# Causal row maxima as whole-array matmuls, one head at a time, beside scores in halves of the array

## What is computed

```python
x = x + layernorm(attention(layernorm(x)))
x = x + layernorm(moe(layernorm(x)))      # 8 experts, 2 per token

# attention, 16 heads of 16 channels, latent keys of 64
c_kv  = x @ W_dkv.T
q_lat = einsum('bhtd,hdl->bhtl', q, k_eff)
attn  = softmax(causal(q_lat @ c_kv.T / 4))
y     = (attn @ c_kv) @ v_eff
```

## Time and profile before

| | us |
|---|---|
| median of 3 runs (lowest, highest) | 1520.93 (1519.54, 1530.33) |
| profiled execution | 1524.09 |
| its span in the profile | 1522.4 |
| mean granted TensorE clock | 0.805 |

### The profile page before, as it was taken

The page is one execution under the profiler, slowest core; times in us unless marked ns, Lnnn a source line. Parts: engine busy times, 40 slices in busy tenths (PEclk is TensorE's granted clock), DMA queues, the critical chain, the costliest instruction groups (busy, mean ns, idle before and its releaser), DMA issues. The chain is left out here.

```text
span 1522.4 us, 26952 instructions
## 1 busy us (share of the span) xinstructions
PE 1097.4 (72%) x8321; PEld 771.1 (51%) x8322; DVE 812.4 (53%) x2076; ACT 644.2 (42%) x1112; POOL 526.3 (35%) x544
## 2 busy tenths in 40 slices
PE   6843678888888888889872350799999999998000
PEld 3421344344434434444322350799899899998000
DVE  4522656655665666555507851455455555555255
ACT  3430045554554555455562441344344444444322
POOL 3100045544554454444454776100000000000785
PEclk9985579988996898777895555899999999999555
DMA  4974225533553445443342124423441432411324
GB/s 154 282 199 144 93 71 183 178 133 126 184 187 106 153 148 178 149 151 109 130 174 113 55 73 148 157 64 137 153 156 48 153 118 81 155 41 48 94 85 152
DMA packets 109100, 200.27 MB, mean 132 GB/s; under 512 B 27396, under 2 KB 76948, under 8 KB 100756
## 3 DMA queue, kind: packets, MB, share of 16 engines
q1 hardware_dynamic: 96488, 143.74, 29.0%
q0 software_dynamic: 12544, 55.62, 10.2%
HBM read 109.38 MB, written 89.42 MB: 131 GB/s over the span
## 5 line engine op out<-in xcount | busy, mean ns | idle before, releaser
L782 ACT ACTIVATE att_pt<-att_ps_s 128x1024 f32<-128x1024 f32 (+3 forms) x384 | 293.9, 813 | 270.6 <-PE att_ps_s L700 269.3
L812 DVE TENSOR_REDUCE att_pm<-att_ps_m 128x1 f32<-128x512 f32 (+1 forms) x512 | 306.5, 650 | 183.6 <-PE att_ps_m L652 110.9
L1430 ACT ACTIVATE moe_hf<-moe_ps_h,moe_b 128x256 f32<-128x256 f32 x288 | 137.2, 476 | 237.3 <-PE moe_ps_h L1381 232.1
L596 POOL TENSOR_SCALAR_AFFINE_SELECT att_pt<-att_pt 128x512 f32<-128x512 f32 x128 | 80.9, 638 | 321.7 <-ACT att_pt L782 321.7
L652 PE MATMUL att_ps_m<-att_k,att_q 50*128 50x512 f32 (+3 forms) x576 | 174.2, 437 | 21.3 <-DVE att_pm L812 11.1
L700 PE MATMUL att_ps_s<-att_q,att_k 50*128 50x512 f32 (+3 forms) x576 | 137.5, 443 | 41.5 <-ACT att_pt L782 30.9
L717 PE MATMUL att_ps_o<-att_pt,att_v 128*17 128x512 f32 (+3 forms) x1152 | 142.3, 618 | 8.1 <-POOL att_pt L596 4.3
L1456 DVE TENSOR_TENSOR moe_hTl<-moe_hf,moe_hTh 128x256 fp32r<-128x256 f32 x288 | 122.6, 426 | 9.8
L700 PEld LDWEIGHTS att_ps_s<-att_q,att_k 50*128 50x128 f32 x576 | 62.7, 198 | 122.8 <-issue 63.8
L652 PEld LDWEIGHTS att_ps_m<-att_k,att_q 50*128 50x128 f32 x576 | 90.5, 212 | 67.0 <-DVE att_pm L812 50.9
L586 POOL TENSOR_TENSOR att_rec<-att_sums,att_minus 128x16 f32<-128x16 f32 x33 | 96.0, 2909 | 39.1 <-ACT att_sums L768 39.1
(11 more groups left out here) (195 smaller groups left out, 2483.9 us busy)
## 6 DMA issues: line engine op xcount, KB each, us to landing
att_raw<-in_w SPq DMA_DIRECT2D x16, 1024.0 KB, 6.0
ws<-att_raw_hi SPq DMA_DIRECT2D x16, 1024.0 KB, 4.2
ws<-att_raw SPq DMA_DIRECT2D x16, 1024.0 KB, 6.7
ys<-att_zeros SPq DMA_DIRECT2D x16, 640.0 KB, 7.3
moe_rows<-xs SPq DMA_DIRECT2D x38, 256.0 KB, 2.7
ys<-moe_o SPq DMA_DIRECT2D x36, 256.0 KB, 2.2
weights_w_0h<-ws POOLq DMA_DIRECT2D x8, 1024.0 KB, 7.6
weights_w_0l<-ws POOLq DMA_DIRECT2D x8, 1024.0 KB, 10.1
```

The costliest lines, as they stand in the source:

```text
L782: act.activation(pt[:, blk % NPT, 2 * p:2 * p + 2, off:CH], ps_s[k % 2][:, :, off:CH], ACT.Exp, scale=HS ** -0.5).then_inc(ex_done, 1)
L812: return dve.tensor_reduce(pm[:, g % 2, place, h:h + 1], src, AX.X, ALU.max)
L1430: act.activation(hf[:, f % NHB], ps_h[f % NHB][:], ACT.Relu, bias=b1[r][:, f:f + 1]).then_inc(hf_done, 1)
```

## The change

- k has one tile per head (`[P, GH, T]` instead of `[P, 2, T]`), with the other head's 64 rows and the unused rows zero. q stays two heads to a tile, so one matmul over all 128 rows gives one head's products. All q and k slots are zeroed once: slot 0 in `project` (GpSimd q, VectorE k), slots 1 to 3 by GpSimd at the start of `attend`. SP waits for `init` of a slot before it loads into it.
- A unit is one matmul per piece and head over 128 rows, and its mask one bf16 matmul, identity 128 x 128 by 128 columns.
- Units are dealt one by one, by a cost per step. The turn goes from step 17 to step 16.
- Scores keep their two halves, reading k at `2 * p + e`.
- `xf` is no longer held during attention; its four loads are issued by SP in `route`, one after the other, and `residual` waits for each.

The steps that have units, before (pairs) and after, counted through both planners: before, steps 0, 1, 2, 5, 7 to 11, 13 to 17, 19, 20 and 22, with ten units in steps 14 to 17; after, steps 0, 2, 3, 4, 6, 7, 8, 10, 11, 12, 14, 15, 16, 18, 19, 20, 22 and 23, with four units in steps 14 to 17 and nine in 22, 23 and 0.

```diff
@@ add_slot
-    slots["k"].append(s.sb(f"k{g}", [P, 2, T], F32R))
+    slots["k"].append(s.sb(f"k{g}", [P, GH, T], F32R))
@@ load_group
-                         (kg[r:r + 2 * HS, h // 2, :], ks[:, c]), (kg[r + 2 * HS:r + KR, h // 2, :], ks[0, c])):
+                         (kg[r:r + 2 * HS, h, :], ks[:, c]), (kg[r + 2 * HS:r + KR, h, :], ks[0, c])):
@@ project
+                                                  (slots["q"][0][:].bitcast(F32), 0.0))):
...
+                dve.memset(slots["k"][0][:].bitcast(F32), 0.0).then_inc(slots["init"][0], 1)
@@ bank_jobs
+MATMUL, VALUES, SWITCH, MASK = 0.235 / CH, 0.44 / CH, 0.2, 0.125
...
+    work = [("unit", 1, m) for m in range(HALF, NU)] + [("unit", 2, m) for m in range(HALF)]
+    cost = [unit_keys(m) * MATMUL + len(UNITS[m][0]) * MASK * any(k0 + keys == (i + 1) * P for i, k0, keys, _ in UNITS[m][1])
+            for _, _, m in work]
+    taken = [2 * (CH - past(k)) * MATMUL for k in range(NS)]
+    for k in range(1, NS, 4):
+        taken[k] += SWITCH + sum((CH - past(2 * (blk % NB))) * VALUES for blk in (k // 2 - 2, k // 2 - 1))
+    even = (sum(taken) + sum(cost)) / NS
+    room = [max(0, even - t) for t in taken]
...
-    out[17] += [("turn", 1, 0), ("turn", 1, 1)]
+    out[16] += [("turn", 1, 0), ("turn", 1, 1)]
@@ attend, sync
                 for g in range(1, NSL):
+                    sp.wait_ge(slots["init"][g], 2)
                     load_ones(sp, d, slots, g)
...
-                        if g == 1:
-                            sp.dma_start(keep["xf"][:, bass.ds(b * TB, TB)],
-                                         d["x"][bass.ds(b * T, T), :].rearrange("(k p) c -> p k c", p=P)
-                                         ).then_inc(xf_in, 16)
@@ attend, gpsimd
+                for g in range(1, NSL):
+                    pool.memset(qg[g][:].bitcast(F32), 0.0).then_inc(slots["init"][g], 1)
+                    pool.memset(kg[g][:].bitcast(F32), 0.0).then_inc(slots["init"][g], 1)
@@ attend, tensor: unit replaces units
+                        for h in heads:
                             diag = k0 + keys == (i + 1) * P
...
+                            ins = pe.matmul(out[:, end:end + keys], qg[slot][:, h // 2, i * P:(i + 1) * P],
+                                            kg[slot][:, h, k0:k0 + keys], start=True, stop=not diag)
+                            end += keys
                             if diag:
...
+                                ins = pe.matmul(out[:, end - P:end], identb[:], future[:], start=False, stop=True)
@@ scores
-                        ins = pe.matmul(out[:, e, off:CH], kg[slot][rows, p, j * P:(j + 1) * P],
+                        ins = pe.matmul(out[:, e, off:CH], kg[slot][rows, 2 * p + e, j * P:(j + 1) * P],
@@ route, sync and vector
+                for b in range(B):
+                    sp.dma_start(xf[:, b * TB:(b + 1) * TB], d["x"][b * T:(b + 1) * T, :].rearrange("(k p) c -> p k c", p=P)
+                                 ).then_inc(xf_in, 16)
+                    sp.wait_ge(xf_in, b * 16 + 16)
...
                 def residual(b):
+                    dve.wait_ge(xf_in, b * 16 + 16)
```

More of the change, by code:

```diff
@@ L412, in unit_keys, with past @@
     return len(heads) * sum(keys for _, _, keys, _ in pieces)
+MATMUL, VALUES, SWITCH, MASK = 0.235 / CH, 0.44 / CH, 0.2, 0.125
+def past(k):
+    c, j, _ = STEPS[k]
+    return max(0, (j - c * TC) * P)
 def bank_jobs():
-    work = [("unit", 1, m) for m in range(HALF, NU, 2)] + [("unit", 2, m) for m in range(0, HALF, 2)]
-    cost = [2 * unit_keys(m) + 128 for _, _, m in work]
-    width = [CH - max(0, (j - c * TC) * P) + 96 for c, j, _ in STEPS]
+    work = [("unit", 1, m) for m in range(HALF, NU)] + [("unit", 2, m) for m in range(HALF)]
[6 more added lines that the diff above has]
+    room = [max(0, even - t) for t in taken]
     out, step, done = [[] for _ in STEPS], 0, 0
-    for (kind, more, m), c in zip(work, cost):
-        while step < NS - 1 and (done + c / 2) / sum(cost) > sum(width[:step + 1]) / sum(width):
+    for job, c in zip(work, cost):
+        while step < NS - 1 and (done + c / 2) / sum(cost) > sum(room[:step + 1]) / sum(room):
             step += 1
-        out[step] += [(kind, more, m), (kind, more, m + 1)]
+        out[step].append(job)
         done += c
@@ L634, in free, with unit @@
                         pe.wait_ge(bank_read[n % NBK], turns(b, n))
-                def units(b, g, m, n):
-                    pieces = UNITS[m][1]
+                def unit(b, g, m, out):
+                    heads, pieces = UNITS[m]
                     slot = g % NSL
@@ L641, in units @@
                         pe.wait_ge(loaded[slot], at(b, g // NSL * NSL, LOADS, NSL * LOADS + ONES))
-                    at_col, last = 0, [None, None]
+                    end = 0
                     for i, k0, keys, _ in pieces:
-                        for pair in range(len(UNITS[m][0])):
+                        for h in heads:
                             diag = k0 + keys == (i + 1) * P
-                            end = at_col + keys
-                            for e in range(2):
-                                h = UNITS[m + e][0][pair]
-                                rows = slice(64 * e, 64 * e + KM)
-                                if at_col == 0:
-                                    free(b, n + e)
-                                last[e] = pe.matmul(ps_m[(n + e) % NBK][:, at_col:end], qg[slot][rows, h // 2, i * P:(i + 1) * P],
-                                                    kg[slot][rows, h // 2, k0:k0 + keys], start=True, stop=not diag)
-                            if diag:
-                                for z in range(2):
-                                    for e in range(2):
-                                        rows = slice(64 * e, 64 * e + 64)
-                                        col = end - P + z * (P // 2)
-                                        last[e] = pe.matmul(ps_m[(n + e) % NBK][:, col:col + P // 2], pick[rows, z], future[rows, z],
-                                                            start=False, stop=z == 1)
-                            at_col = end
-                    for e in range(2):
-                        last[e].then_inc(bank_made[(n + e) % NBK], 1)
+                            ins = pe.matmul(out[:, end:end + keys], qg[slot][:, h // 2, i * P:(i + 1) * P],
+                                            kg[slot][:, h, k0:k0 + keys], start=True, stop=not diag)
+                            end += keys
+                            if diag:
+                                ins = pe.matmul(out[:, end - P:end], identb[:], future[:], start=False, stop=True)
+                    return ins
                 def max_turn(b, g, half, out):
@@ L681, in jobs @@
                     for (kind, more, m), n in todo:
-                        if kind == "unit":
-                            if m % 2 == 0:
-                                units(b, g + more, m, n)
-                            continue
                         free(b, n)
-                        do = {"turn": max_turn, "out": turn_out}[kind]
+                        do = {"unit": unit, "turn": max_turn, "out": turn_out}[kind]
                         do(b, g + more, m, ps_m[n % NBK]).then_inc(bank_made[n % NBK], 1)
@@ L1585, in build @@
         keep = {"ident": s.sb("ident", [P, P]), "passed": s.sem("passed"),
-                "pick": s.sb("pick", [P, 2, P], BF16), "future": s.sb("future", [P, 2, P // 2], BF16)}
+                "identb": s.sb("identb", [P, P], BF16), "future": s.sb("future", [P, P], BF16)}
         keep["y"] = s.sb("y", [P, B * NG + 1, TB, GH * HS])
-        keep["xf"] = s.sb("xf", [P, TILES, C])
         with ExitStack() as inner:
-            slots = {part: [] for part in ("q", "k", "v", "loaded")}
+            slots = {part: [] for part in ("q", "k", "v", "loaded", "init")}
             add_slot(slots, Store(nc, inner, "slots"), 0)
@@ L1595, in build @@
             attend(nc, d, keep, slots)
+        keep["xf"] = s.sb("xf", [P, TILES, C])
         keep["wgt"] = s.sb("wgt", [P, 3, TILES])
@@ L1617 @@
     w = {k.replace("L0_attn_", "").replace("L0_ffn_", ""): np.asarray(a) for k, a in inputs.items()}
-    half = P // 2
-    pick = np.zeros((half, 2, P), np.float32)
-    future = np.zeros((half, 2, half), np.float32)
-    pick[:, 0, :half] = np.eye(half)
-    future[:, 0] = np.triu(np.full((half, half), -1e30), 1)
-    pick[:half - 1, 1, half:P - 1] = np.eye(half - 1)
-    pick[half - 1, 1, :half] = 1.0
-    future[:, 1] = future[:, 0]
-    future[half - 1, 1] = -1e30
+    future = np.triu(np.full((P, P), -1e30, np.float32), 1)
     arrays = {
```

23 lines of the change are left out of this document (12 added, 11 removed).

## The result

The changed kernel takes 1536.05 us (median of 15 runs, 1532.67 to 1545.41), the kernel before 1527.99 on the same chips (median of 15, 1519.54 to 1533.86). The ratio is 1.0064, 95% interval 1.0043 to 1.0084: slower by 0.4 to 0.8%, less than the 1% by which the prediction counts a change. The forecast was 1531.0 against 1520.9, +0.66%.

A forecast was written before the change was run, and what follows sets the result against it. No one engine is full: TensorE carries the chain, ScalarE and VectorE hold it up in turn. From 1524.1 us, loop 0, start +6.0, routing +4.5 give 1534.6; the median is 3.2 lower, 1531; range 1482 to 1573.

The forecast's parts named there:

- Change 1: Attention loop: whole-row units cost TensorE 8.5 us a group, 4.2 more than before, and masks 3.8, 1.2 more.
- whole-row units of 512 columns every 0.22 to 0.24: Attention loop: spacing in us of such units on TensorE, listed among the signs that the forecast is right.
- Change 2: Attention loop: each step with units changes between halves and whole rows and back, 0.25 us a step, 4.5 a group.
- The row of four transposes: Attention loop: four transposes plus the change to values take 0.59 us; put one change of shape at 0.11 to 0.35.
- Rival B: Attention loop: changes of shape cost 0.35 a step, clock stays 0.83, groups take 41 us: 1565 us, chance 0.25.
- Change 3: Attention loop: units dealt singly remove waits inside pairs; group 36.5 us at full clock, clock 0.93, 38.6 in all, as before.
- the back edge: Attention loop: the jump back stops TensorE's issue; three of 3.5 us over 14 groups, 0.75 a group.
- late max rows: Start of groups in the attention loop: waits for max rows fall from 9.7 us to 3, 0.4 a group.
- Change 4: Zeroing q and k: slot 0 is covered and free; SP's wait for slot 1 delays attention's first scores by 6.0 us.
- Change 5: Routing: x loaded after attention lands at 815 to 816.5, first use at 810.8; +4.5 us, between 0 and 10.
- Rival A: Attention loop: the clock stays up, groups take 35.8 us and the loop gives back 39: 1492 us, chance 0.28.
- Rival C: Attention start and routing: the zeroing and x's load do not show: 1521 us, chance 0.07.

The follow-up runs named there:

- a_scores_whole: Changed kernel with its scores also over all 128 rows, so no change of shape between scores and units: 1517.0 us, ratio 0.9944 to the kernel before.
- a_nomask: Changed kernel without the 32 causal mask matmuls of a group's max units: 1523.4 us, ratio 0.9992 to the kernel before.
- a_olddeal: Changed kernel with units and turn in the places of the planner before: 1536.7 us, ratio 1.0076 to the kernel before.
- b_places: Kernel before with its units still as pairs in halves, but put in the new planner's places: 1584.1 us, ratio 1.0392.
- c_order_xfirst: a_scores_whole with raw weights fetched during zeroing, first max rows ahead of group 2's loads, x's first load ahead of routing's constants: 1510.2 us, ratio 0.9901.
- b_xf_late: Kernel before with only the load of x moved behind attention: 1528.5 us, ratio 1.0031.
- c_split_wlate: a_scores_whole with k of slots 1 to 3 zeroed by VectorE and the experts' first weights issued after the first x lands: 1514.5 us, ratio 0.9918.

## Why the prediction was right, and where its steps were not

The time, the sign and the places were right. By its steps:

- **Change 1, whole rows.** The streaming price, 0.06 for 128 columns and 0.23 for 512, is what units show in a_scores_whole where nothing stands before them. In after the promised sign "whole-row units of 512 columns every 0.22 to 0.24" failed: none passes in under 0.31. The units' line has 14.5 us a group, not 8.5. By the starts in the clean group the 6.0 us between them are, as an estimate: 2.0 for the change of shape ahead of 18 first units, 0.5 for that behind the five units that scores follow, 1.7 for 19 units behind a mask (0.09 each), and the rest, about 2, units that follow VectorE, which needs 0.68 for each of 512 columns; their loads wait 2.1 us for it. So what the sum called waits, 3.1, stands in part in this line and not among PE's own waits, and most of the excess is no wait. The mask, 0.12 in the sum, costs 0.13 between short units; 0.07 is what its removal gives net in a_nomask.
- **Change 2, changes of shape.** 4.5 us a group forecast, 4.9 found net (a_scores_whole), and 0.23 a step by single starts where 0.25 was taken. The row of four transposes, taken at its lower end, was the right neighbour. The planner before also gives units to step 4, so it has 18 such steps and not 17; nothing hangs on it. Rival B's premise, 0.35 a step, fell with it.
- **Change 3, the deal.** A group at the full clock was 36.8 for 36.5, the clock 0.95 for 0.93, the loop even within 2.4 us: sizes right. The reason did not hold. I wrote that the deal "removes the waits inside pairs" and thins out VectorE's crowd. a_olddeal shows that the deal is worth nothing here and that the heavier TensorE work removed the waits, and b_places that on its own the deal costs 58 us. The terms beside the 36.5 were off and cancel: the back edge was counted three times and is two jumps, 3.5 us each, as the earlier trace rows had; late max rows, 0.4 a group, did not come; and the 0.9 for the clock does not follow from the 0.93 taken (0.07 x 38.6 is 2.7, the time lost at half speed). The four groups that hold low stretches are together 16 us longer than clean ones, 1.15 a group.
- **Change 4, the zeros.** +6.0 forecast; 6.5 from attention's start to the first scores, of which 6.0 is SP's wait. The first scores stand at 204 instead of the promised 201, since projection also ended 2.5 us later. That the zeros of slot 0 are covered holds: the first matmul still waits for the last weights, at 10.26 us (10.94 in the earlier trace rows).
- **Change 5, x after attention.** Forecast +4.5, found +8.3 at the residual and +6.2 at the experts' first matmul. The failed step is the landing time, taken from the earlier trace rows (8.5 to 10.0 us in the loop): behind 4 MB of weights it is 12.9, and c_order_xfirst shows the order as the cause. That max rows in the loop would be less late held (9.7 us, then none), and b_xf_late ties it to x.
- **Rival A** (clock up, 1492) had its mechanism but not its price: 36.8 us at the full clock in place of 35.8, and four groups of 14 that run at 0.84 to 0.87 for part of their time. **Rival C** fell on both its parts. **Rival B** was right that TensorE has no slack left, and wrong that the clock would stay at 0.83.

That the sum came within 2 us of the measured difference (10 forecast, 8 between the medians) is in part luck: x was 1.7 to 3.8 us too cheap and the clean group 0.3 (4 us over 14), while late rows (5.6 over 14 groups) and one back edge (3.5) were counted and did not come.

## What to carry to other kernels

Scores or products that alternate between halves of the rows and whole rows paid 0.23 to 0.27 us per excursion here; where operands are zero-padded anyway, streaming the zeros in both (here 9,216 columns a group more) was cheaper than changing shape. Judge a deal of side work together with the load of the engine that takes it: the same places were worth nothing where TensorE was full and cost 2.5 to 4% where it had slack, and the granted clock, not the busy column, told so. When a load moves to another stage, look at what is issued ahead of it on all queues, and put no wait ahead of an independent instruction that someone else needs.

## What the runs showed of the hardware that was not expected

- The granted clock answered to the places of the same work: 0.83 over 14 groups before, 0.72 with the pairs of units moved (b_places), at equal instruction counts (3,694 and 3,695). In b_places it falls twice in most groups, near the third and near the tenth step.
- The clock of the changed kernel fell once without any visible cause: the group from 592 to 634 shows the same instructions as its neighbours and runs at 0.84, taking 42.3 us instead of 36.8. Such a fall is no single accident: in a_olddeal every second group begins with one, at 280, 437 and 594 with no back edge before it, and TensorE is recorded busy without a gap there (second row).

```profile
592.00:634.00 42.00, 41.11 (x233) 19.89 (x233) 23.09 (x42) 21.12 (x29) 18.76 (x16) 0.84 0.41 141
...
593.00:608.00 15.00, 15.00 (x71) 7.05 (x69) 6.36 (x10) 5.80 (x9) 4.17 (x3) 0.54 0.53 155
```

- The Trainium skill's "TensorE: Matmul & The Clock Gate", Part 1, has the clock throttled by default and released by activity. That more work brought more of the upper level (0.83 to 0.95, and 0.98 in a_scores_whole), and less work less (0.93 in a_nomask), agrees with it. The falls at 592 and in a_olddeal stay open.
- A transfer of 1 MB took 5.4 us alone (c_split_wlate) and 12.9 us issued after 4 MB of others (after); issued just ahead of the same 4 MB it took 5.8 (c_order_xfirst).
- Behind a bf16 mask a whole-row unit of 128 columns took 0.15 us, and 0.06 behind whole-row scores (a_scores_whole).
